# 16-head attention inside a transformer: the masking writes negated scaled scores and accumulates their minimum

## The reference

```
scores = einsum('bhqd,bhkd->bhqk', q, k) * 64 ** -0.5 + causal      # A1: K and V shared by 4 heads
att    = where(causal, q k^T * 64 ** -0.5, -inf) - FF[:, None]       # A2: FF is one running sum for all heads
att    = where(keep[:, None], att, -inf)                             # A2: keeps a fifth of the keys of each query
y      = softmax(att) @ v
```

## Time and profile before

| | |
|---|---|
| time, median of 3 runs | 3847.53 us (3843.65 to 3848.81) |
| the profiled execution | 3843.2 us, its span 3841.6 us |
| TensorE matmul busy | 3112.1 us, 81% |
| VectorE busy | 2395.1 us, 62% |
| ScalarE busy | 1960.6 us, 51% |
| POOL busy | 1328.2 us, 35% |
| mean granted TensorE clock | 0.92 of full speed |

### The profile page before, as it was taken

One profiled execution on the slowest core, in us unless ns is written; L12 is line 12 of the kernel. 1 busy time (PEld: TensorE's weight loads), 2 busy tenths in 40 slices (PEclk: granted clock), 3 DMA queues, 4 the chain that ended last, 5 costly groups with the idle time before them and its releaser, 6 DMA issues. The chain is left out here.

```text
span 3841.6 us, 48726 instructions
## 1 busy us (share of the span) xinstructions
PE 3112.1 (81%) x17780; PEld 2035.9 (53%) x17780; DVE 2395.1 (62%) x4521; ACT 1960.6 (51%) x4372; POOL 1328.2 (35%) x1068
## 2 busy tenths in 40 slices
PE   4886888888787788888878769888886877988887
PEld 2444447775244545777535344577743534467773
DVE  3357369994245637999415653899931565399983
ACT  1435257773253526777225352777622544277762
POOL 0213056670021306766003120766500312086740
PEclk9998989999898998999989889799998988989998
DMA  3000100000200010000110001000011000100001
GB/s 124 1 1 1 41 17 1 1 1 23 67 1 1 1 47 12 1 1 1 58 31 1 1 1 58 1 1 1 1 58 31 1 1 1 58 1 1 1 1 60
DMA packets 69640, 68.19 MB, mean 18 GB/s; under 512 B 6491, under 2 KB 49907, under 8 KB 69254
## 3 DMA queue, kind: packets, MB, share of 16 engines
q1 hardware_dynamic: 60288, 56.15, 4.8%
q10 hardware_dynamic: 9094, 8.72, 0.7%
HBM read 63.81 MB, written 1.05 MB: 17 GB/s over the span
## 5 line engine op out<-in xcount | busy, mean ns | idle before, releaser
L1308 POOL TENSOR_TENSOR arena<-arena 128x1536 f32<-128x1536 f32 (+9 forms) x480 | 1020.6, 2161 | 438.5 <-DVE arena L1367 326.3
L1189 PE MATMUL psum<-ident,arena 128*128 128x128 f32 (+7 forms) x7168 | 873.6, 280 | 241.6 <-ACT arena L1284 227.6
L1189 PEld LDWEIGHTS psum<-ident,arena 128*128 128x128 f32 (+7 forms) x7168 | 795.9, 138 | 354.6 <-ACT arena L1284 258.0
L1274 ACT ACTIVATE arena<-arena 128x64 f32<-128x64 f32 (+7 forms) x2048 | 707.9, 484 | 140.6 <-PE psum L1198 140.6
L1367 DVE TENSOR_TENSOR arena<-arena,psum 128x1536 f32<-128x1536 f32 (+9 forms) x480 | 494.0, 1061 | 54.8 <-ACT arena L1284 47.1
L1353 DVE TENSOR_TENSOR arena<-arena,psum 128x1536 f32<-128x1536 f32 (+9 forms) x480 | 493.6, 1061 | 8.2 <-POOL arena L1308 6.3
L473 POOL TENSOR_TENSOR rstd<-veps,mhalf 128x4 f32<-128x4 f32 x32 | 32.4, 1011 | 1280.7 <-DVE veps L464 1280.7
L763 POOL TENSOR_SCALAR arena<-arena 128x512 f32<-128x512 f32 (+3 forms) x512 | 263.8, 532 | 589.3 <-DVE arena L735 589.3
L1284 ACT ACTIVATE arena<-arena 128x1536 f32<-128x1536 f32 (+2 forms) x288 | 406.0, 1415 | 116.9 <-DVE arena L1353 116.8
L692 ACT ACTIVATE arena<-arena 128x512 f32<-128x512 f32 (+3 forms) x512 | 281.8, 552 | 268.7 <-DVE arena L730 268.4
L649 PE MATMUL psum<-ident,arena 128*128 128x128 f32 x1280 | 192.8, 295 | 148.4 <-ACT arena L703 89.1
(11 more groups left out here) (207 smaller groups left out, 3959.2 us busy)
## 6 DMA issues: line engine op xcount, KB each, us to landing
stream<-in_L_ffn_W SPq DMA_DIRECT2D x160, 256.0 KB, 3.1
arena<-in_L_ffn_h_w SPq DMA_DIRECT2D x8, 1024.0 KB, 8.4
arena<-in_L_ffn_w_w SPq DMA_DIRECT2D x12, 256.0 KB, 4.5
arena<-in_L_ffn_h_w ACTq DMA_DIRECT2D x2, 1024.0 KB
wa<-in_L_attn_W_attn ACTq DMA_DIRECT2D x1, 1536.0 KB
wq<-in_L_attn_Wq ACTq DMA_DIRECT2D x2, 512.0 KB
wo<-in_L_attn_Wo ACTq DMA_DIRECT2D x2, 512.0 KB
x<-in_L_attn_x SPq DMA_DIRECT2D x4, 256.0 KB, 3.7
```

The costliest lines, as they stand in the source:

```text
L1189: last = nc.tensor.matmul(ps[ch.half][0:rows, to:to + P], buf[:, c:c + rows], ident[:], start=first, stop=False, is_transpose=True, skip_g ...
L1274: nc.scalar.activation(by_key[:, 0:HD - r, j], keys[:, h, 0:HD - r], ACT.Exp, bias=NB[:, j:j + 1], scale=Q3[tt % 2][:, j:j + 1]).then_inc( ...
L1308: last = nc.gpsimd.tensor_tensor(of_piece(D3[n % 5], piece), q, keys_on(K3[tt % 2], k, nk, w), ALU.mult)
```

## The change

In both attentions the masking instruction now computes -1/8 times (scores + mask) and accumulates the minimum of that, which is -1/8 times the maximum of before, straight into `nb`. The exponential has the scale -1 with the same bias. L730, VectorE's wait for the whole group before it, and ScalarE's wait for `negmax` go; ScalarE waits instead before each unit's exponential until that unit is masked.

```diff
                 if t < A.ng:
                     g = A.groups[t]
-                    act.wait_ge(s["negmax"], t + 1)
                     for j in range(g.pairs):
                         for half in range(2):
                             pr, u = two(PRG[t % 4])[:, half, g.cols(j)], g.u0 + 2 * j + half
-                            nc.scalar.activation(pr, pr, ACT.Exp, bias=nb[:, u:u + 1], scale=HD ** -0.5,
+                            act.wait_ge(s["masked"], u + 1)
+                            nc.scalar.activation(pr, pr, ACT.Exp, bias=nb[:, u:u + 1], scale=-1.0,
                                                  accum_out=rsum[:, u:u + 1]).then_inc(s["probs"], 1)
...
                             nc.vector.tensor_tensor_reduce(out=two(PRG[t % 4])[:, half, g.cols(j)],
                                                            in0=GS[t % 2][:, half, g.cols(j)], in1=mask,
-                                                           scale=1.0, scalar=-BIG, op0=ALU.add, op1=ALU.max,
-                                                           accum_out=mx[:, u:u + 1]).then_inc(s["masked"], 1)
-                    dve.wait_ge(s["masked"], g.end)
-                    nc.vector.tensor_scalar(nb[:, g.u0:g.end], mx[:, g.u0:g.end], -HD ** -0.5, None, ALU.mult)\
-                        .then_inc(s["negmax"], 1)
+                                                           scale=-HD ** -0.5, scalar=BIG, op0=ALU.add, op1=ALU.min,
+                                                           accum_out=nb[:, u:u + 1]).then_inc(s["masked"], 1)
```

## The result

The changed kernel took 3778.43 us (median of 6 runs, 3778.24 to 3781.51), against 3847.82 us before (6 runs): a ratio of 0.9821, with a 95% interval of 0.9811 to 0.9832. The forecast was 3777.5. The profiled execution took 3778.54 us, its span 3777.0.

The account below looks back on a forecast made before the run. No engine is full and limits differ by stage; loops over engines hold groups. Gains of 9.8 us in A1 and 7.7 in A2 make 17.5 per batch element, times four 70, off the 3847.5 median: 3777.5 us, range 3765 to 3800.

Parts of the forecast that it names:

- What waits: Both attentions: ScalarE's exponentials (L692) waited 268.4 us for the negation L730; their wait for VectorE would fall to about 140.
- The early start: A1's 512-key groups: the first exponential waits only for its own unit, 0.74 us after masking instead of 1.55.
- TensorE takes over in A1: A1's 512-key groups: scores-to-transposes falls from 4.78 to 3.97 us, under TensorE's own 4.21; 3.13 per group instead of 3.41.
- the second window: A1's 128- and 256-key groups: gain 5.1 us per batch element, 3.9 over the 128-key groups and 1.2 over the 256-key.
- VectorE in A2: A2's 512-key groups, bound by VectorE: masking repeats every 3.78 us instead of 3.98, 0.2 saved per group.
- at the two places where VectorE waits for scores: A2's 512-key groups: 1.2 us gained there besides 7 times 0.2, together 2.6 per batch element.
- Rival C: TensorE's granted clock rises to 1.00 in two windows and gives 14 us more, 3764 us; chance 0.15.
- All four batch elements repeat it: Both attentions: one batch element's gain of 17.5 us was worked out and multiplied by four to 70 us.
- The forms, at nothing: Masking with addition, minimum and real scale, and exponential scale -1, cost 0; bounds 0.05 us less to 0.35 more.
- The 336 further waits, at nothing: ScalarE's additional unit-wise waits cost 0, all but a group's first satisfied ahead; bound 0.04 to 0.12 us each.
- The median against the profile: Whole kernel: profiled 3843.2 us less 70 would be 3773; predicted on the median of runs, 3847.5, it is 3777.5.
- Rival A's price: Only the instruction's own length returns: 0.1 us in 136 loop-bound groups, 0.2 in 40 VectorE-bound, 22 us, 3825; chance 0.12.

Follow-up runs that it names:

- the third experiment: The kernel before with only the new masking form (minimum, real scale) and exponential scale -1, negation replaced by a copy, waits as before: 3845.91 us, ratio 0.9998.

## Why the prediction was right

- *What waits.* L692's wait of 268 us did mark the place. It fell to 196, not to 140 as I wrote. That number was not worked out from the schedule. Two thirds of what remains is in A2, more than half of that with VectorE still pruning.
- *The early start.* Forecast 0.74 us from masking to the first exponential, measured 0.73 and no gap behind it. That it is the main cause is shown from both sides: without it (group wait) 31 of 69 us, with it but all of VectorE's old work 64 by the ratio. How much of the 31 is VectorE's shorter turn and how much the clock was not separated.
- *TensorE takes over in A1.* Forecast 3.13 us for each 512-key group, measured 3.11; for 384 keys 2.52 against 2.46 (masking at 154.34, 156.80, 159.26). The small surplus of the first window is this. In the second window the forecast was 5.1 and the measured gain 4.9, but not for the forecast's reasons. The window from the first 128-key to the first 512-key masking took 25.0 us before; in the third batch element, where the clock didn't fall there, it took 23.5. So 1.5 of the 4.9 are the clock's, and the schedule gave 3.4: 1.7 over the 128-key groups, where the forecast had 3.9, and 1.8 over the 256-key groups, where it had 1.2.
- *VectorE in A2.* Forecast every 3.78, measured 3.79. The forecast's 1.2 us "at the two places where VectorE waits for scores" came at one place, the fifth group: 5.27 fell to 3.79. Beyond the 0.2 that VectorE saves, this is the clock's earlier rise. It came with the group wait too, and stayed away in the same program where the clock rose late (5.08).
- *Rival C, the clock, came true in part beside the forecast.* The sum has no term for it. The granted clock went from 0.93 to 1.00 in A1's second window and from 0.75 to 0.84 in A2's first. My estimate from the steps above is 3 to 4 us in A1 and 4 in A2, over all elements: some 8 of the 70 us.
- *"All four batch elements repeat it".* They don't quite: the gains run from 18.4 us in the first to 16.0 in the third, which differs from the others in its clock. The forecast of 17.5 for each met their mean.
- *The forms, at nothing.* Shown by the third experiment.
- *The 336 further waits, at nothing.* Exponentials of 512 keys within a group start 0.72 us apart, as before.
- *The median against the profile.* I took 70 from the median of the runs. The stages gave 70.1 in the profiles, and medians differ by 69.4. The 5.5 us given back in the profile are offset by the profiled execution of before, which lay 4.6 under the median of all six. The hit to 1 us owes much to luck: the schedule gave less than the sum says, and the clock, which the sum leaves out, made it up.
- *Rival A's price* was too low by the medians, 22 for 31. Its sum of 0.1 and 0.2 a group left out TensorE's clock, which no longer fell in A1's groups and rose earlier in A2; this accounts for part of the miss.

## What to carry to other kernels

Price an instruction by who waits behind it, not by its busy time: 30.8 us of negations held back 69, more than twice their length, since each also made a whole group a barrier. Where a producer works unit by unit, let the consumer wait unit by unit; here this cost nothing, since a unit was masked every 0.61 us and exponentiated every 0.72. To size it, find the loop that closes over two or more engines in the timeline, subtract, and stop at the next engine's own work; the sum over stages came out within 0.6 us in each of seven windows, though in at least two of them the clock had a part that the sum didn't know. Before trusting such a hit, compare the rounds of the loop within one trace: where the same instructions take different times, something else than the schedule is at work.

## What the runs showed of the hardware

- A VectorE instruction that must wait for an accumulator's read of the same engine started 0.12 us after the read started; one that needn't started with it (213.60 and 213.72 before, 293.35 and 293.47 with the multiplication and its wait, 290.27 twice without the wait). In a loop that VectorE bounds, the wait made 3.86 us into 3.97.
- TensorE's granted clock fell to the lower level after three of four waits of 2.96 to 2.98 us behind the first 128-key group, and stayed at the full one after the fourth and, with the group wait, after 2.64 in the same place. In the third element it fell after waits of only 0.50 and 1.51 us, where the same waits left it at full in the first. A fall of 3.4 us cost the stage 1.1 to 1.2 us.
- The same program can therefore take different times for the same work in different rounds of its loop: A2's stage took 143.1 us in one round and 141.2 in the others, with a rise of the clock some 6 us later.
- One execution of the changed kernel had ScalarE's 2048 short exponentials at 498 ns on average, another at 483, and each kept to its level in all four batch elements (496 to 501 and 482 to 485). The other profiles have 483 to 487.
